# Passes 8 and 9 of a graph network kernel: four tiles of eight gathered by TensorE instead of three

## What is computed

```python
# L2: maximum over the edges of a node
msg = inputs[src] * timestamp
h = jax.ops.segment_max(msg, dst, num_segments=n)
# L3, twice (NREPEATS = 2)
W = (jax.nn.relu(edgefeats @ fnet_w1 + fnet_b1) @ fnet_w2 + fnet_b2).reshape(-1, 16, 16)
xj = hx[edge_src]
m = jnp.einsum('ei,eio->eo', xj, W)
agg = jax.ops.segment_sum(m, edge_dst, num_segments=n) * inv_deg[:, None]
hx = _gru_cell(agg, hx, ...)
```

## Time and profile before

| | |
|---|---|
| median of 3 runs | 9585.77 us |
| lowest, highest | 9583.65, 9609.09 us |
| the profiled execution | 9624.08 us, span 9622.1 us |
| mean granted TensorE clock over the span | 0.915 |
| busy, share of the span | PE 91%, PEld 66%, DVE 73%, ACT 38%, POOL 51% |
| indirect DMAs of passes 7 to 9 on POOL | 3030 |
| loads of `src_parts` | 606 of 192 KB |

### The profile page before, as it was taken

How to read it: one execution, slowest core, us unless ns; L and a number is a source line. 1 busy time by engine, 2 the same in 40 slices (tenths; PEclk the granted TensorE clock), 3 DMA queues, 4 the chain that set the end, 5 groups by cost and what they waited for, 6 DMA issues and landing times.

```text
span 9622.1 us, 208480 instructions
## 1 busy us (share of the span) xinstructions
PE 8789.0 (91%) x72187; PEld 6327.8 (66%) x72191; DVE 7010.4 (73%) x13550; ACT 3702.5 (38%) x10806; POOL 4954.2 (51%) x4703
## 2 busy tenths in 40 slices
PE   1599999999976999997699999998999998999998
PEld 0366666666524975976477777776777776777776
DVE  2488899999742123122378777777999998999998
ACT  5245444444320002000144444444555554555554
POOL 0588788788750000000175555544777663777662
PEclk9999999999955987987689888888999998999998
DMA  8633333333218864967732222222222221222221
GB/s 303 234 92 101 115 105 105 104 104 103 71 58 338 326 240 185 345 239 283 270 65 65 64 64 64 64 64 47 54 54 53 53 54 42 53 54 54 53 54 36
DMA packets 869111, 1162.86 MB, mean 121 GB/s; under 512 B 269846, under 2 KB 751298, under 8 KB 868118
## 3 DMA queue, kind: packets, MB, share of 16 engines
q1 hardware_dynamic: 674612, 1078.18, 33.9%
q0 software_dynamic: 150336, 28.94, 3.7%
q10 hardware_dynamic: 43426, 45.70, 1.5%
HBM read 1018.14 MB, written 133.22 MB: 120 GB/s over the span
## 4 chain that ended last, share of the span: by engine, by line
PE 66%; DVE 17%; issue 7%; DMA 5%; SPq 4%; ACT 1%; DVEq 0%; ACTq 0%
PE ps L830 16%; PE ps L711 14%; PE ps L909 9%; PE ps L700 6%; DMA arena<-adj 5%; PE ps L788 4%; PE ps L847 3%; SPq L576 3%; DVE arena L1995 3%; DVE dinv L1995 3%; PE ps L720 2%; DVE dinv L1457 2%; DVE invdeg L1457 2%; PE ps L983 2%; PE ps L795 2%
## 5 line engine op out<-in xcount | busy, mean ns | idle before, releaser
L657 POOL DMA_INDIRECT arena<-tab,x_all x3030 | 2939.7, 970 | 3700.1 <-DMA tab<-stage 2239.4
L675 POOL DMA_INDIRECT adj<-acc x1616 | 1960.8, 1213 | 560.2 <-issue 471.5
L909 PE MATMUL ps<-arena 128*128 128x192 bf16 (+1 forms) x16464 | 1167.9, 234 | 172.0 <-DMA arena<-adj 171.3
L909 PEld LDWEIGHTS ps<-arena 128*128 128x128 bf16 x16464 | 1118.2, 103 | 229.8 <-DMA arena<-adj 198.7
L711 PE MATMUL ps<-dinv,acc 112*128 112x384 bf16 x6363 | 1163.8, 342 | 44.0 <-DVE acc L1485 43.5
L1105 ACT ACTIVATE wide<-ps,not_all 128x256 bf16<-128x256 f32 x1616 | 741.0, 485 | 1197.3 <-PE ps L795 1197.3
L711 PE MATMUL ps<-invdeg,acc 112*128 112x384 bf16 x6363 | 1173.7, 344 | 2.8 <-issue 2.8
L1277 ACT ACTIVATE arena<-w_iota,rel 128x128 f32<-128x128 f32 x3232 | 988.8, 388 | 13.1
L711 PEld LDWEIGHTS ps<-dinv,acc 112*128 112x128 bf16 x6363 | 642.1, 104 | 523.7 <-issue 182.3
L711 PEld LDWEIGHTS ps<-invdeg,acc 112*128 112x128 bf16 x6363 | 645.0, 105 | 492.4 <-issue 155.4
L1621 DVE TENSOR_TENSOR arena<-hot_a,threes 128x1024 bf16<-128x1024 bf16 x606 | 738.4, 1218 | 0.0
(11 more groups left out here) (314 smaller groups left out, 14116.1 us busy)
## 6 DMA issues: line engine op xcount, KB each, us to landing
arena<-adj SPq DMA_DIRECT2D x588, 896.0 KB, 6.9
x_all<-src_parts SPq DMA_DIRECT2D x606, 192.0 KB
arena<-rels SPq DMA_DIRECT2D x202, 512.0 KB
arena<-tab SPq DMA_DIRECT2D x1616, 64.0 KB
adj<-zero SPq DMA_DIRECT2D x28, 3136.0 KB, 27.5
arena<-rT SPq DMA_DIRECT2D x404, 128.0 KB
arena<-tab,x_all POOLq DMA_INDIRECT x3030
adj<-acc POOLq DMA_INDIRECT x1616
```

The source lines that it names most:

```text
L657: pool.indirect_dma_start(G[b][:, u, :], None, TABLE[PHASES[p]], bass.IndirectOffsetOnAxis(ap=idx[:, t:t + 1], axis=0)).then_inc(gathered[ ...
L675: pool.indirect_dma_start(adj_cells, bass.IndirectOffsetOnAxis(ap=pair[:, t, 0:1], axis=0), pair16[:, t, 2:3], None).then_inc(celled[g], 16)
L909: last = mm(ps[:, 2 * par + u // 2, u % 2 * W:(u % 2 + 1) * W], ring[i][:, s, u * P:(u + 1) * P], rows[:, j * SC + s, :, :].rearrange("p k ...
```

## The change

The number of tiles that TensorE gathers becomes a function of the pass, `by_pe`: four in passes 8 and 9 (`GT` = 4, `GC` = 512), three in pass 7. POOL fetches the rest, four and five (`by_pool`). Every buffer of the on-chip gather is laid out for four tiles, and pass 7 leaves out the first of them (`skipped`), so its operations keep their sizes; only its loads of `src_parts` grow, from 192 to 256 KB, as those of passes 8 and 9 do. `parts_row` moves onto the columns of `src_g` and `src_t`, which are no longer in use by then.

```diff
--- before.py
+++ after.py
@@ -60,9 +60,8 @@
 M = NS * P // GR
 BANK_BLOCKS = 25
 CHUNKS = ((0, 4), (4, 7))
-GT = 3
+GT = 4
 GC = GT * P
-FETCHED = HT - GT
 AHEAD = 3
 STRIPS = 4
 SE = HE // STRIPS
@@ -86,6 +85,21 @@
     ("l2_W", (16, 16)), ("l2_b", (16, 1)), ("f1", (13, 32)), ("fb1", (32, 1)), ("w2b", (33, 256)),
     ("w_ih", (16, 48)), ("w_hh", (16, 48)), ("b_ih", (16, 3)), ("b_hh", (16, 3)),
 ]
+
+
+def by_pe(p, k):
+
+    return GT - 1 if p == 7 else GT
+
+
+def by_pool(p, k):
+
+    return HT - by_pe(p, k)
+
+
+def skipped(p, k):
+
+    return GT - by_pe(p, k)
 class Steps:
@@ -170,12 +184,12 @@
         picked_by = [dinv[:, 2 * HE + (2 * BL + i * GT) * P:2 * HE + (2 * BL + (i + 1) * GT) * P] for i in range(2)]
         HOT8 = 2 * HE + (2 * BL + 2 * GT) * P
         hot8 = [(dinv if i == 0 else invdeg)[0:BLANES, o:o + BL * GC // 2].bitcast(bf16).rearrange("p (b e) -> p b e", b=BL)
-                for i, o in enumerate((HOT8, 5120))]
+                for i, o in enumerate((HOT8, 4864))]
         src_g, src_t = [x_all[0:T // TR, 1664 + i * 2 * GC:1664 + (i + 1) * 2 * GC].bitcast(i32) for i in range(2)]
         src_16 = [x_all[0:T // TR, 1664 + (4 + i) * GC:1664 + (5 + i) * GC].bitcast(f16) for i in range(2)]
-        PARTS0 = 1664 + 6 * GC
+        PARTS0 = 1664
         parts_row = [x_all[:, PARTS0 + i * GC:PARTS0 + (i + 1) * GC].bitcast(f16) for i in range(SL)]
-        CONST0 = PARTS0 + SL * GC
+        CONST0 = 1664 + 6 * GC
         lane_b, lane_a = x_all[:, CONST0:CONST0 + BL], x_all[:, CONST0 + 8:CONST0 + 9]
         lane_i = x_all[:, CONST0 + 9:CONST0 + 10].bitcast(i32)
         pick_f = x_all[:, CONST0 + 16:CONST0 + 32]
@@ -379,7 +393,8 @@
         def gather_count(p, k):
             s = k % len(G)
-            return 16 * FETCHED * ((p - 7) * len(range(s, NB, len(G))) + k // len(G) + 1)
+            whole = sum(by_pool(q, b) for q in range(7, p) for b in range(s, NB, len(G)))
+            return 16 * (whole + sum(by_pool(p, b) for b in range(s, k + 1, len(G))))
         def part_count(p, j):
@@ -624,7 +639,7 @@
                 if p == 6:
                     nodes_done(sp, 6)
                     sp.dma_start(src_g.rearrange("r (i e) -> r i e", i=2),
-                                 a["src_r"][0].rearrange("(r i e) -> r i e", i=2, e=HE)[:, :, FETCHED * P:]).then_inc(src_in, 16)
+                                 a["src_r"][0].rearrange("(r i e) -> r i e", i=2, e=HE)[:, :, (HT - GT) * P:]).then_inc(src_in, 16)
                     sp.dma_start(bias_row, a["w2b"][32:33, :].to_broadcast([P, 256])).then_inc(bias_in, 16)
                 block_loads(p)
             sp.wait_ge(parted, PARTED)
@@ -652,7 +667,7 @@
                     pool.wait_ge(vec[p].sem, vec[p].at(0, 0))
                 else:
                     pool.wait_ge(vec[p].sem, vec[p].at(max(k - len(G) - 1, -SL), MSG))
-                for u in range(FETCHED):
+                for u in range(by_pool(p, k)):
                     t = k * HT + u
                     pool.indirect_dma_start(
                         G[b][:, u, :], None, TABLE[PHASES[p]],
@@ -706,9 +721,10 @@
                 pe.wait_ge(hot8_made[p], j + 1)
                 pe.wait_ge(selected[p], j)
                 pe.sem_inc(pe_go, 1)
+                lo = skipped(p, j) * P
                 for b in range(BL):
                     for i in range(3):
-                        last = mm(picked_rows, x8[:, b, i, :], hot8[j % 2][:, b, :],
+                        last = mm(picked_rows[:, lo:], x8[:, b, i, :], hot8[j % 2][:, b, lo:],
                                   start=b == i == 0, stop=b == BL - 1 and i == 2)
                 last.then_inc(picked[p], 1)
@@ -716,7 +732,7 @@
                 pe.wait_ge(selected[p], j + 1)
                 pe.wait_ge(copied[p], j)
-                for u in range(GT):
+                for u in range(skipped(p, j), GT):
                     last = mm(turned_rows[:, u * 16:(u + 1) * 16], picked_by[j % 2][:, u * P:(u + 1) * P], pick_f,
                               start=True, stop=True)
                 last.then_inc(turned[p], 1)
@@ -1309,7 +1325,8 @@
             def copy8(p, j):
                 act.wait_ge(turned[p], j + 1)
-                act_fn(G[j % len(G)][:, FETCHED:, :], turned_rows.rearrange("p (u f) -> p u f", f=16),
+                act_fn(G[j % len(G)][:, by_pool(p, j):, :],
+                       turned_rows[:, skipped(p, j) * 16:].rearrange("p (u f) -> p u f", f=16),
                        ACT.Copy).then_inc(copied[p], 1)
             def open_one_hots(p, r):
@@ -1453,8 +1470,9 @@
                 dve.wait_ge(parts_in[j % SL], part_count(p, j))
                 if j >= 2:
                     dve.wait_ge(picked[p], j - 1)
+                lo = skipped(p, j) * P
                 for b in range(BL):
-                    last = ts(hot8[j % 2][:, b, :], parts_row[j % SL][0:BLANES, 0:GC], lane_b[0:BLANES, b:b + 1], None,
+                    last = ts(hot8[j % 2][:, b, lo:], parts_row[j % SL][0:BLANES, lo:GC], lane_b[0:BLANES, b:b + 1], None,
                               ALU.is_equal)
                 last.then_inc(hot8_made[p], 1)
@@ -1463,7 +1481,9 @@
                 dve.wait_ge(picked[p], j + 1)
                 if j >= 2:
                     dve.wait_ge(turned[p], j - 1)
-                stt(picked_by[j % 2], parts_row[j % SL][:, GC:], lane_a[:, 0:1], picked_rows, ALU.is_equal, ALU.mult
+                lo = skipped(p, j) * P
+                stt(picked_by[j % 2][:, lo:], parts_row[j % SL][:, GC + lo:], lane_a[:, 0:1], picked_rows[:, lo:],
+                    ALU.is_equal, ALU.mult
                     ).then_inc(selected[p], 1)
             def select_ahead(p, k):
@@ -1990,7 +2010,7 @@
                     for q in range(4):
                         dve.wait_ge(ten[p].sem, ten[p].at(k, WT8))
-                        if q == FETCHED // 2:
+                        if q == by_pool(p, k) // 2:
                             dve.wait_ge(copied[p], k + 1)
                         tt(products[h][:, q * 512:(q + 1) * 512].rearrange("p (u o i) -> p u o i", u=2, i=16),
                            ps[:, 4 + q, :].rearrange("p (u o i) -> p u o i", u=2, i=16),
```

## The result

| | before | after |
|---|---|---|
| median of 3 runs | 9585.77 us | 10138.41 us |
| lowest, highest | 9583.65, 9609.09 us | 10111.02, 10142.96 us |
| ratio, 95% interval | | 1.056 (1.053 to 1.059) |
| span of the profiled execution | 9622.1 us | 10136.4 us |
| mean granted clock | 0.915 | 0.921 |

A forecast was written before the change was run, and what follows sets the result against it. TensorE and DVE were taken as tied at about 7.1 us a batch, with TensorE alone leading afterwards. Loops +519, openings +12 and loads +4 gave +535 us on the 9586 us median: 10121 us, range 10065 to 10200.

The forecast's parts named there:

- The tie: Loops of passes 8 and 9 before: TensorE needs 7.09 us a batch without slack, DVE 7.10 us, both full.
- The gather: TensorE's 21 gather matmuls, 384 to 512 columns: cost goes by columns, 0.42 ns each, so 1.12 us more a batch.
- The turn: TensorE's turn in passes 8 and 9, three products to four: 0.23 us more a batch.
- The batch: Loops of passes 8 and 9: TensorE alone sets the pace at 8.44 us a batch, +519 us over both loops.
- DVE: One-hot rows +0.3 us and selection +0.14 us a batch: DVE needs 7.5 us, at most 7.9, below TensorE's 8.44.
- POOL: Four fetches for five in passes 8 and 9: POOL, read as having a third of its time free, gains nothing.
- The openings: Starts of passes 8 and 9, where TensorE and DVE take turns: +6.2 us each, +12 us together.
- term of 2.0: First gather of a pass in the openings, running at the lower clock of 1.2 GHz: 2.0 us longer.
- The loads: Larger loads of parts delay the openings of passes 7, 8 and 9: +4 us; up to 60 in pass 7 if uncovered.
- the first: Rival: the clock falls in passes 8 and 9, at 0.88 +455 us on top, 10576 us; chance 6%.
- The second rival, DVE's pace: TensorE has slack and DVE sets the batch at 7.5 or 7.9 us: 9750 to 9910 us; chance 3%.
- The third, POOL's relief: Instruction cost is fixed and fewer POOL fetches speed DVE's one-hot rows: -40 us, 9546 us; chance 1%.

## Why the prediction was right

It said 10121 us, 10065 to 10200, and 10138 was measured; it said why, and the runs bear out the steps that carry the sum. Two smaller readings were off, the opening and POOL's free time. That the median comes as near as 17 us is in part luck: passes 8 and 9 gave 525 us where 531 were forecast, and the rest is scatter ahead of them.

- **The tie.** Its base was that TensorE had no slack in 7.09 us, read from one row of the first batch. The run with DVE at 256 columns shows it directly: 7.09 us with DVE waiting. The run with the gather at 256 shows the other side: shorter gathers, next to nothing gained, DVE at 7.05 us.
- **The gather.** 0.42 ns a column from 384 and 392 columns, so 1.12 us a batch. Measured 4.53 - 3.41 = 1.12.
- **The turn.** 0.23 forecast and measured; taking it out gave 0.22 back.
- **The batch.** 8.44 forecast, 8.43 measured (1669.8 us for 198, pass 8 from 6633.76 to 8303.56). The loops give +516 for the +519 forecast.
- **DVE.** 7.5 us forecast, 7.55 measured where it leads. The one-hot rows went from 1.68 to 2.06, 0.38 for 0.3 taken and between the bounds of 0.2 and 0.56; the selection +0.13 for 0.14. DVE's share is 0.91, in the 0.89 to 0.94 said. None of it is on the path, as the run with DVE at 384 shows.
- **POOL.** Nothing gained, forecast; 46 us busy in 100 for the 47 said. The run with the fetch left out puts the gain at some 10 us. But "a third of its time free" was a misreading of 67 to 76 us busy in 100. Without any pause POOL is busy for 76, as the run with two tiles shows; five fetches at 1.27 us are 6.3 of 7.13 us, so about a tenth was free. The sum does not hang on it, since what was free was enough.
- **The openings** were mis-sized: +5 each for 6.2. The step from gather to gather is 5.58 as said, but the first one grew by less than 2.0: in pass 8 from 6.64 to 7.15 us, in pass 9 from 6.23 us to

```profile
8371.64 6.54 PE L727 MATMUL ps<-dinv,acc 112*128 112x512 bf16 x21 [16.30 <-DVE acc L1505]
```

  The low rate is as I read it, 0.320 us a matmul with 384 columns and 0.427 with 512, double that of later gathers. But the clock rises within this gather, before the change too, and when it does differs from run to run: in pass 9 after 5.5 us before and 3.8 after. The first gather of pass 9 took 5.24 us in the run with only the larger loads and 7.81 in the run with three products in the turn, with the same sizes as before and after. So a term of 2.0 can't be told from one execution of each kernel.
- **The loads** were forecast at +4 us, with part of a reserve of 60 in the range; they cost nothing that the run with them alone can show.
- **The rivals.** The clock stayed at 1.00 in both loops, so the first did not come: the longer dense part with no waits did not lower it here. By the Trainium skill, "TensorE: Matmul & The Clock Gate", section "A second HAM failure mode: psum-queue depth-cycling", it could have; that rule did not show in the changed kernel. It fell here where the gathers were shorter and TensorE waited for DVE besides (two tiles in every batch: 0.88; 256 columns: 0.98 over the loops). The second rival, DVE's pace, would have needed slack that is not there. The third, POOL's relief, is real in kind and small: the Trainium skill, "GPSIMD Engine Reference", section "Key points", names the sharing, and one fetch of five less gave 4.9 and 4.5 us a pass here.

Against the profiled execution the forecast was 10159 and the new one took 10138: the 21 us missing are, to 1 us, pass 7's scatter (-23), the stages ahead of it (+12), the openings (-2), the loads (-4) and the loops (-3).

## What to carry to other kernels

Before work is moved to an engine, look whether it waits for anything itself: two engines can each be busy for the whole of a batch and be tied, and then a cut on either gives nothing while an addition on either costs its full length. The place to tell is a batch in which the other engine can't be the reason, such as the first of a loop. An engine that waits for the others is not a bottleneck, however many small transfers it issues, and relieving it is worth only what its neighbours suffer from it. How much it has left is not its idle share: POOL's 76% was all it could do, and what tells is who ends its idle time.

## What the runs showed that was not expected

- DVE's comparison of 16-bit rows with one scalar does not cost in proportion: seven of 256, 384 and 512 elements took 1.45, 1.68 and 2.06 us.
- Less work on TensorE came with a lower granted clock: with gathers of 256 columns and a wait of some 1 us a batch for DVE it went from 1.00 to 0.98 with three tiles in the turn and on DVE, and to 0.88 with two tiles throughout. In neither run did TensorE set the pace of passes 8 and 9, so what the clock cost is not shown; DVE's waits for the matrices rose from 1 us a loop to 11 and to 81 and 84. Why the two runs differ so much in clock is open.
- POOL at its full pace shows as 76% busy, since 0.30 us lie between two of its fetches.
- On one chip all kernels took some 21% longer, with idle time between instructions and a lower clock. The one kernel that ran both there and elsewhere had a ratio of 1.004 (1.002 to 1.007) there and 0.998 (0.997 to 1.000) elsewhere, so an effect of a per cent measured on such a chip should not be carried to another.
